# Biases ahead of positions, batch 0's logits in the loop, the pick in two parts and projections by 128 rows, in a recurrence, top-k and attention kernel

## The reference

```
a = tanh(x @ WA.T); b = x @ WB.T            # 16 states
h_t = a_t * h_(t-1) + b_t                   # restarts every batch
g = sigmoid(x @ Wg.T + bg); dx = x @ WD.T + bD
x = layernorm(x + (h @ WC.T) * g + dx * (1 - g))

weights = x @ router_w + router_b           # one logit per token
the 511 tokens with the largest weights, in order of position:
  hn = rmsnorm(x_sel, ln1); q, k, v = hn @ wq, wk, wv; rope(q), rope(k)
  attention with 16 heads of 16, causal mask picked by row and by column
  x1 = x_sel + o @ wo; x2 = x1 + gelu(rmsnorm(x1, ln2) @ w1) @ w2
  row of out = x2 * weight
x = layernorm(x + out + x * (1 - selected))
```

## Time and profile before

| what | us |
|---|---|
| median of 3 runs | 549.7 (548.16 to 550.84) |
| profiled execution, its own time | 546.17 |
| its span, first to last instruction | 544.4 |
| PE busy, matmuls | 444.0 (82%) |
| DVE busy | 392.7 (72%) |
| ACT busy | 293.5 (54%) |
| POOL busy | 185.7 (34%) |

### The profile page before, as it was taken

One profiled execution on the slowest core, in us unless ns is written; L12 is line 12 of the kernel. 1 busy time (PEld: TensorE's weight loads), 2 busy tenths in 40 slices (PEclk: granted clock), 3 DMA queues, 4 the chain that ended last, 5 costly groups with the idle time before them and its releaser, 6 DMA issues.

```text
span 544.4 us, 10299 instructions
## 1 busy us (share of the span) xinstructions
PE 444.0 (82%) x3346; PEld 329.2 (60%) x3346; DVE 392.7 (72%) x1218; ACT 293.5 (54%) x612; POOL 185.7 (34%) x218
## 2 busy tenths in 40 slices
PE   0379999999999533379798999997998999996980
PEld 0258778888888322345575666674585666673560
DVE  0357798888888788729568999947567999946050
ACT  1234546555564440024776999945577999942300
POOL 8015767676767650275940000001000000001432
PEclk9979999999999855559898999999999999998995
DMA  9601332424331210066650000000000000000100
GB/s 248 193 0 40 120 114 78 153 80 125 108 107 48 78 39 1 20 225 235 224 148 2 1 4 0 1 2 2 0 1 1 2 3 0 2 1 1 40 23 17
DMA packets 29846, 33.85 MB, mean 62 GB/s; under 512 B 6340, under 2 KB 25448, under 8 KB 29800
## 3 DMA queue, kind: packets, MB, share of 16 engines
q1 hardware_dynamic: 23024, 24.78, 14.1%
q0 software_dynamic: 3520, 8.40, 5.1%
q10 hardware_dynamic: 3256, 0.10, 0.5%
HBM read 19.63 MB, written 13.63 MB: 61 GB/s over the span
## 4 chain that ended last, share of the span: by engine, by line
PE 44%; DVE 11%; issue 4%; ACT 4%; POOL 2%; POOLq 1%; DVEq 0%; ACTq 0%
PE ps L871 10%; PE ps L887 6%; PE ps L941 5%; PE ps L858 5%; PE ps L948 4%; PE ps L808 3%; PE ps L834 3%; PE ps L827 2%; PE ps L744 1%; PE ps L812 1%; DVE arena L1325 1%; DVE arena L1532 1%; PE ps L793 1%; PE ps L766 1%; DVE qk L1335 1%
## 5 line engine op out<-in xcount | busy, mean ns | idle before, releaser
L1133 ACT ACTIVATE arena<-arena,nmax 128x511 f32<-128x511 f32 x128 | 92.0, 720 | 8.0 <-DVE nmax L1532 7.3
L1532 DVE CUSTOM_DVE_ANT_0 arena<-ps,nmask 128x511 f32<-128x511 f32 x128 | 84.8, 683 | 0.5 <-DVE nmask L1475 0.2
L871 PE MATMUL ps<-ident,arena 128*128 128x128 f32 x512 | 79.7, 278 | 3.5 <-ACT big L391 1.1
L871 PEld LDWEIGHTS ps<-ident,arena 128*128 128x128 f32 x512 | 60.3, 142 | 24.7 <-ACT arena L1133 14.5
L623 POOL COPY arena<-v_sb 128x256 f32<-128x256 f32 (+1 forms) x8 | 3.2, 398 | 155.3 <-PE ps L887 155.3
L676 PE MATMUL ps<-wgd_hi,x_hi 128*128 128x512 f32 x128 | 51.6, 403 | 0.0
L391 DVE COPY big<-ps 128x512 f32<-128x512 f32 x64 | 44.0, 688 | 9.9 <-PE ps L871 9.4
L858 PE MATMUL ps<-arena 96*128 (+1 forms) x128 | 49.3, 391 | 1.8 <-DVE nmask L1475 0.8
L678 PE MATMUL ps<-wgd_hi,x_lo 128*128 128x512 f32 x128 | 50.5, 395 | 0.0
L677 PE MATMUL ps<-wgd_lo,x_hi 128*128 128x512 f32 x128 | 50.4, 394 | 0.0
L485 POOL TENSOR_TENSOR arena<-arena 128x512 f32<-128x512 f32 x32 | 41.3, 1292 | 5.4 <-DVE arena L1226 3.6
(11 more groups left out here) (230 smaller groups left out, 1015.5 us busy)
## 6 DMA issues: line engine op xcount, KB each, us to landing
arena<-in_L_attn_x SPq DMA_DIRECT2D x16, 512.0 KB, 4.5
out<-ob_sb SPq DMA_DIRECT2D x16, 512.0 KB, 3.2
w_sb<-in_L_ffn_w SPq DMA_DIRECT2D x2, 1024.0 KB, 11.1
mt_scratch<-nmask SPq DMA_DIRECT2D x8, 256.0 KB, 2.6
mt_scratch<-big SPq DMA_DIRECT2D x8, 256.0 KB, 2.2
big<-in_L_attn_Wg SPq DMA_DIRECT2D x1, 256.0 KB
big<-in_L_attn_WD SPq DMA_DIRECT2D x1, 256.0 KB
wqk<-in_L_ffn_wq SPq DMA_DIRECT2D x1, 256.0 KB, 8.0
```

What stands on the lines that cost most here:

```text
L871: mm = pe.transpose(ps[:, 2 + u % 2, k * P:(k + 1) * P], pr[u % 4][:, k * P:(k + 1) * P], ident[:, :])
L1133: act.activation(pr[u % 4][:, 0:K - 1], sm[u % 4][:, 0:K - 1], ACT.Exp, bias=nmax[:, c, h:h + 1], scale=-1.0, accum_out=rsum[:, c, h:h + 1 ...
L1532: dve.tensor_tensor_reduce(sm[u % 4][:, 0:K - 1], ps[:, S_BANKS[u % AHEAD], 0:K - 1], nmask[b][:, c, 0:K - 1], 1.0, 3.4e38, ALU.add, ALU.m ...
```

## The change

It has these parts (line numbers are those of before):

- The four bias transfers get a semaphore of their own and stand right behind `WC` in ACT's queue; PE's first weight transposes wait for seven transfers. Positions are loaded by ACT in group 1 of the loop, between `round_h(2)` and `gate(1, 1)`.
- `recurrence_inputs(0)` stands ahead of tile 1's transposes; DVE splits the weights in four wider instructions, makes `scan(0)` ahead of the constants and the low part of tile 1's second half behind them; group 0's `gates` stand ahead of tile 2's transposes.
- `positions` moves from group 2 to group 6; batch 0's `logits` (DVE, end of group 9), `factors` (POOL, group 9) and `split_values` (POOL, group 10) stand in the loop.
- `pick` is cut in `pick_rows` (2 of 15 values) and `pick_rest` (13); `rows` needs the first alone, a new `factors` on DVE takes the rest. `pick_rest(1)` stands between PE's first and second projected chunk.
- Normalising, turning and projecting go chunk by chunk from each gather on. Batch 1's first two chunks are projected between the two batches' mask rows, which are turned through four banks.
- Two of ACT's four split copies go to POOL (`more_copies`), and POOL's queue behind the row and mask row gathers becomes as in the diff.
- Some pairs of semaphores become one that counts on.

```diff
 # POOL
-                if G == 2:
+                if G == 6:
                     positions()
+                if G == NG + 1:
+                    factors(0)
+                if G == NG + 2:
+                    split_values(0)
...
-            for b in range(B):
-                factors(b)
-            for b in range(B):
-                split_values(b)
+            factors(1)
+            split_values(1)
...
+            def more_copies(b, c):
+                q, k = (e_sb[c % 2][:, m, :, :, :] for m in range(2))
+                pool.wait_ge(e_parts, 2 * (c + b * C) + 2)
+                pool.tensor_copy(q[:, :, 1, :], q[:, :, 3, :])
+                pool.tensor_copy(k[:, :, 2, :], k[:, :, 3, :]).then_inc(e_ready[2], 1)
...
             gather_x(1)
             gather_mask_rows(1)
+            for c in range(2):
+                more_copies(0, c)
+            gather_mask_columns(0)
+            for c in range(2, C):
+                more_copies(0, c)
+            gather_mask_columns(1)
             for b in range(B):
                 first_sum(b)
             for b in range(B):
                 kept(b)
-            for b in range(B):
-                pool.wait_ge(mT_stored[b], 16 * M_STORES)
-                for c in range(C):
-                    gather(m_k[b][:, c, :], mt_dram[b], row_t[:, b, c:c + 1], m_k_in[b])
 # PE
+                if G == 0:
+                    pe.wait_ge(split_ready, 2 * KD + 1)
+                    pe.wait_ge(const_ready, 1)
                 pe.wait_ge(h_lo_ready, G + 1)
...
-            pe.wait_ge(w_loaded, 16 * 11)
+            pe.wait_ge(w_loaded, 16 * 7)
...
-            for b in range(B):
-                pick(b)
+            pick_rows(0)
+            pick_rest(0)
+            pick_rows(1)
...
-            turn_hn(0, 0)
-            project(0, range(C))
+            turn_first_hn(0, 0)
+            turn_first_hn(0, 1)
+            project(0, range(1))
+            pick_rest(1)
+            for c in range(1, C):
+                if c + 1 < C:
+                    turn_first_hn(0, c + 1)
+                project(0, range(c, c + 1))
             turn_mask_rows(0)
+            for c in range(2):
+                turn_first_hn(1, c)
+            for c in range(2):
+                project(1, range(c, c + 1))
+                turn_first_hn(1, 2 + c)
             turn_mask_rows(1)
-            turn_hn(1, 0)
...
             for c in range(C):
                 turn_split(0, c)
-                project(1, range(c, c + 1))
+                if c < 2:
+                    project(1, range(2 + c, 3 + c))
 # ACT
+                if G == 1:
+                    load_positions()
                 if G < NGB:
                     gate(G, 1)
...
-                    act.wait_ge(e_parts, 2 * done + 2)
-                    act.copy(q[:, :, 1, :], q[:, :, 3, :])
-                    act.copy(k[:, :, 2, :], k[:, :, 3, :]).then_inc(e_ready[1], 1)
 # DVE
+                if G == NG + 1:
+                    logits(0)
...
             angles(0)
-            dve.wait_ge(x_sel_in[0], 16 * C)
-            first_normalised(0)
+            for c in range(2):
+                first_normalised(0, c)
+            rows(1)
+            for c in range(2, C):
+                first_normalised(0, c)
+            factors(1)
             cosines(0)
             for c in range(C):
                 value(0, c)
                 rope(0, c)
-            dve.wait_ge(x_sel_in[1], 16 * C)
-            dve.wait_ge(hnT_done[0], KD)
-            first_normalised(1)
-            split(0, lambda c: value(1, c))
+                if c == 0:
+                    angles(1)
+                if c == 1:
+                    parts(0, 0)
+                if c == 2:
+                    for n in range(C):
+                        first_normalised(1, n)
+            parts(0, 1)
+            for c in range(2):
+                value(1, c)
+            for c in range(C):
+                copy_turned(0, c)
+                if c < 2:
+                    parts(0, 2 + c)
+                    value(1, 2 + c)
             copy_mask()
```

More of the change, by code:

```diff
@@ L626, in _ @@
                 all_turns(pool, turn_body)
-                rsqrt(ms[b][:, 5, :], ms[b][:, 4, :], ms_ready[b], 1, rms_ready[b])
+                rsqrt(ms[b][:, 5, :], ms[b][:, 4, :], ms_ready, b + 1, rms_ready)
+                if b < B - 1:
+                    for c in range(C):
+                        more_copies(b + 1, c)
             for b in range(B):
@@ L820, in turn_split @@
                 done = c + b * C
-                for n in range(2):
+                for n in range(3):
                     pe.wait_ge(e_ready[n], done + 1)
@@ L1036, in normalise, with load_positions @@
                 last.then_inc(ob_ready, 1)
+            def load_positions():
+                with nc.allow_non_contiguous_dma("positions by token"):
+                    for b in range(B):
+                        act.dma_start(pos_tok[:, b, :], pos_in[b].rearrange("(n p) -> p n", p=P)).then_inc(pos_loaded, 16)
+                        act.dma_start(pos_last[:, b, :], pos_in[b:b + 1, MS - 1:MS].broadcast_to((P, 1))).then_inc(pos_loaded, 16)
             copy_xT(0, 0)
@@ L1044, in _ @@
                 act.copy(wgd_hi[:, c, :], ps[:, 3 + c, :]).then_inc(wt_copied, 1)
-            for c in range(KD):
-                copy_xT(1, c)
+            copy_xT(1, 0)
             decays(0)
+            copy_xT(1, 1)
             round_h(0)
@@ L1304, in _ @@
[L1304 removed]
             def logits(b):
+                dve.wait_ge(dve_step, step.k)
                 step.link(dve.scalar_tensor_tensor(q1[:, b, :], minus_mean[:, b, :], sum_rw[:, :], dots[:, b, :],
@@ new lines, in _ @@
+            for c in range(KD):
+                dve.wait_ge(wt_copied, c + 2)
+                dve.tensor_tensor(wgd_lo[:, c, :], ps[:, 3 + c, :], wgd_hi[:, c, :].bitcast(F32),
+                                  ALU.subtract).then_inc(split_ready, 1)
+            rest_of_x(1, 0)
+            scan(0)
+            step.link(dve.tensor_reduce(is_lo[:, 0:1], ident[0:HROWS, N:2 * N], X, ALU.add))
+            step.done(dve.tensor_scalar(is_lo[:, 1:2], is_lo[:, 0:1], -1.0, 1.0, ALU.mult, ALU.add))
+            step.link(dve.tensor_tensor(wc_lo[:, :], ps[0:HROWS, 5, 0:D], wc_hi[:, :].bitcast(F32), ALU.subtract))
@@ new lines, in _ @@
+            dve.tensor_scalar(wc_d[0:HROWS, D:2 * D], wc_r[0:HROWS, :].bitcast(F32), -1.0, None,
+                              ALU.mult).then_inc(const_ready, 1)
+            rest_of_x(1, 1)
+            dve.wait_ge(router_loaded, 32)
+            dve.tensor_copy(ps[:, 1, 0:D], rw_row[:, :])
+            step.done(dve.tensor_reduce(sum_rw[:, :], rw_row[:, :], X, ALU.add))
+            for G in range(NGB + 1):
+                if G > 0:
+                    products(G - 1, 1)
+                    half_statistics(G - 1, 0)
+                if G + 2 < NGB:
+                    rest_of_x(G + 2, 0)
+                if G > 0:
+                    statistics(G - 1)
+                if G < NGB:
+                    products(G, 0)
+                if G + 2 < NGB:
+                    rest_of_x(G + 2, 1)
+                if G + 1 < NGB:
+                    scan(G + 1)
+                if G == NG + 1:
+                    logits(0)
@@ L1406, in _ @@
             one_hots(1)
-            rows(1)
+            factors(0)
             def mean_square(b, sums, out_):
@@ new lines, in copy_turned, with parts @@
+            def copy_turned(b, c):
+                for half in range(2):
+                    dve.wait_ge(eT_done[2 + half], c + b * C + 1)
+                    dve.tensor_copy(qkT[1][:, 8 * half:8 * half + 8, c * P:(c + 1) * P],
+                                    ps[:, :, :].bitcast(BF16)[0:ER, 2 + half, :].rearrange(
+                                        "r (h n) -> r h n", h=8)).then_inc(kT_ready, 1)
+            def parts(b, c):
+                done = c + b * C
+                dve.wait_ge(rope_ready[b], c + 1)
+                for n in range(4):
+                    if done >= 2:
+                        dve.wait_ge(eT_done[n], done - 1)
+                src = qk[b][:, c:c + 1, :].rearrange("p o (m h k) -> p (o m) h k", m=2, h=H)
+                es = e_sb[c % 2]
+                rest = e_rest[:, c % 2, :].rearrange("p (m h k) -> p m h k", m=2, h=H)
+                dve.tensor_copy(es[:, :, :, 0, :], src).then_inc(e_parts, 1)
+                dve.wait_ge(e_parts, 2 * done + 1)
+                step.link(dve.tensor_tensor(rest, src, es[:, :, :, 0, :], ALU.subtract))
+                dve.tensor_copy(es[:, :, :, 3, :], rest).then_inc(e_parts, 1)
+                dve.wait_ge(e_parts, 2 * done + 2)
+                step.done(dve.tensor_tensor(es[:, 0, :, 5, :], rest[:, 0], es[:, 0, :, 3, :], ALU.subtract))
+                dve.tensor_tensor(es[:, 1, :, 4, :], rest[:, 1], es[:, 1, :, 3, :],
+                                  ALU.subtract).then_inc(e_ready[0], 1)
```

347 lines of the change are left out of this document (166 added, 181 removed).

## The result

| | kernel before | changed kernel |
|---|---|---|
| median, us | 549.34 (548.16 to 550.84, 4 runs) | 552.84 (552.28 to 554.89, 4 runs) |
| ratio, 95% interval | | 1.0086 [1.0051, 1.0120] |
| profiled execution, own time / span | 546.17 / 544.4 | 554.89 / 552.6 |

The changed kernel is 3.5 us slower, where 1.6 us faster was forecast: inside the range of 538 to 557, on the wrong side.

What follows compares the result with a forecast made beforehand. PE was taken to bound the loop, chains of small steps the choice and projections. Terms -14.5 + 3.3 + 2.5 - 0.5 + 7.6 = -1.6 us gave 544.6 profiled, 548.1 us median; own range 544.5 to 551.5, overall 538 to 557.

Steps and rivals of the forecast that it cites:

- Start: Kernel start: weights no longer wait for biases and inputs are reordered; -14.5 us (ends -9 and -17).
- The order within the start: Start: first recurrence inputs no longer behind tile 1's transposes; L682 of group 1 at 43.0 instead of 47.08, 4.1 sooner.
- The feared 0.9 of clock: Start: more gaps on PE may put its clock at half again, 0.9 us off the gain.
- Positions in ACT: Loop group 1: ACT's four position issues delay the gate and copies PE needs; +3.3 us (ends 0 and 6.9).
- The groups in the loop: Loop groups 9 and 10: batch 0's logits, factors and value parts cost +2.5 us (ends 0 and 4.2).
- Pick: Row choice: pick_rows at 72 ns a matmul, 1.6 us sooner; pick_rest(1) some 2.1 us, with factors(1) waiting for it.
- Rival D: Pick: pick_rows bound by its 8 columns only, weight loads hidden; 1.5 us sooner than the sum, 546.6 us; chance 0.15.
- Part 5: Projections to attention: POOL's rearranged queue delays L871 from 292.67 to 300.3; +7.6 us (ends +3.5 and +14.2).
- rival B: Ahead of attention: POOL's chain later still, +14.2 us, total 554.7; decides if L871 starts behind 304.6; chance 0.18.
- rival C: Start gives less: WC lands only at 12.9, 4.7 us later than taken; total 552.8 us; chance 0.10.
- the 0.5 behind the loop: Behind the loop: batch 1's logits no longer wait for batch 0's; -0.5 us (ends 0 and -2).

Runs made afterwards that it cites:

- start_alone: Kernel before with only the loads changed (biases ahead, positions loaded by ScalarE in group 1, read in group 6): 0.9848 of the kernel before, 543.12 us.
- loop_out: Changed kernel with logits(0), factors(0) and split_values(0) back behind the loop: 0.9987 of the kernel before, 549.59 us.
- chip E: Later session, no hold: kernel before 544.76 us, the unaltered changed kernel 1.0000 of it.
- chip A: The chip of the first comparison, with a hold: kernel before 549.34 us, changed kernel 1.0086 of it.
- before_fourth: Kernel before, unaltered, run again on a chip with a hold: 550.27 us.
- before_third: Kernel before, unaltered, run again on a chip without a hold: 545.27 us.
- before_again: Kernel before, unaltered, run again on a chip without a hold: 543.96 us.
- late_out: Changed kernel with POOL's multiplies behind the first v_cur copy and batch 0's three steps behind the loop: 0.9724 and 0.9713 without a hold, 0.9844 with one.

## Why the prediction was wrong, point by point

1. *Start.* Forecast -14.5, measured -11.3 at group 1's L709: **3.2 us mis-sized**. WC landed at 9.4, not 8.2, which is 1.2 of it. The order within the start was reckoned at 4.1 and gave 1.5 (start_alone against the changed kernel): 3.6 at the first bias product, and then the two products of group 0 lie 7.5 us apart (24.30 to 31.82) where 5.4 lay before, more given back than the 1.9 taken. The feared 0.9 of clock did not come. (The clock's slices don't show where PE is busy, as the prediction read them: in the first, PE did nothing and the clock stood at 0.9.)
2. *Positions in ACT.* Forecast +3.3, measured +1.5 (the lead over before shrinks from 11.3 to 9.8 us at the next `scales`, 49.08 against 58.91 of the earlier trace rows). In group 1, with the start's loads done, even the long two issues took 0.45 and 0.60.
3. *The groups in the loop.* Forecast +2.5, measured +4.3: 2.8 in the group of `logits(0)` and `factors(0)` instead of 0.7, 1.5 in that of `split_values(0)` (1.8 forecast). loop_out gives 3.9 of it back. The changed kernel in that group, in order of time:

```profile
119.68 1.35 DVE L1326 SCALAR_TENSOR_TENSOR q<-minus_mean,sum_rw,dots 128x32 f32<-128x32 f32 x1
...
119.70 1.28 POOL L489 TENSOR_TENSOR arena<-arena 128x512 f32<-128x512 f32 x1
...
121.68 1.31 POOL L548 TENSOR_TENSOR h_parts<-arena,h_parts 16x512 fp32r<-16x512 f32 x1
...
121.88 1.15 DVE L1335 TENSOR_TENSOR qk<-Wf,qk 128x32 int32<-128x32 int32 x1
```

DVE's L1326 ends at 121.03 and L1335 at 123.03, each just behind the end of the POOL instruction beside it (120.98 and 122.99). Behind the loop the same L1335 took 0.19 and L1326 0.25 (L1333 and L1324 of loop_out). So two of DVE's small steps stood for 2.1 us in all, some half of the 4.3, and DVE was not as idle as its waits for PE let one think. That is read from the rows; no run takes these two waits alone away. The Trainium skill states this (SBUF — State Buffer, "SBUF: two separate sides"): the port pair of the two engines is locked for a whole instruction, also by a VectorE operation with two SBUF inputs against GpSimd's that read SBUF. The trace agrees for the two rows beside GpSimd's operations of 512 columns. It doesn't for one of 8: in loop_out the same two-input operation took 0.19 us at 180.35, inside GpSimd's L498 (179.52, 1.64 us).

4. *Pick.* 32 matmuls with 8 columns took 2.24 us, 70 ns each; 72 were taken. Rival D's rule is out. But `pick_rest(1)` took 3.5 us (230.46) where 2.1 were taken, **1.4 mis-sized**: the 2.1 counted on full clock, and its 52-column matmuls took 109 ns each at a granted clock of 1.00 and 108 at 0.50 (`pick_rest(0)`, 3.47 us in all). The first gather came 1.9 us sooner against the loop's end (-7.0 against -5.0, chip E).
5. **This is the step that failed.** Part 5 let DVE's `factors(1)`, and with it all ropes, wait for `pick_rest(1)` and priced that at the pick's own length, +2.1 us; that the announcement itself could come 8.8 us late was put at nothing. It put the end of chunk 3's second cast at 277.9 in the clock of the kernel before, 2.7 us sooner than 280.57. On chip A it ended at 278.7, which is 284.5 in that clock (5.84 us of lead at the loop's end): 6.6 too late. The hold is what stands in between. Without it, on chip E, the cast came 4.5 us sooner against the loop's end than before, and 2.7 were reckoned. What followed was as forecast: 21.7 us from that cast's start to L916 on chip E and on chip A alike (22.4 from its end were reckoned), with the multiplies at 0.9 each, and PE idle 9.54 (chip A) and 11.94 (D and E). In the clock of the kernel before, L916 started at 305.8 on chip A, behind the 304.6 at which rival B was to decide: **rival B happened**, through a cause that it did not name, and not through a busy DVE, since both groups of eight multiplies took 7.2 and not 9.4. That its 554.7 stood 1.9 above the measured time is luck, and so is that rival C's 552.8 is the measured time: WC landed at 9.4, not at C's 12.9.

Taken without the hold, the errors cancel: start and loop 3.7 us dearer than forecast (-5.0 at the loop's end against -8.7), the way to attention 2.5 cheaper (+4.6 against the loop's end, +7.1 reckoned with the 0.5 behind the loop). The forecast was -1.6 us; -0.4 of span and a ratio of 1.0000 and 1.0005 were measured on E and D. The sum was made on a trace without a hold, of a kernel whose median lay 3.5 us above it. before_fourth, with a hold, is 5.0 and 6.3 us slower than before_third and before_again; that the 3.5 was the hold fits this but has no trace, and the chip of the profiled execution is not on record.

## What to carry to other kernels

Before a queue is rearranged, write down what is behind each moved instruction and who needs it first: 14 us of multiplies that nobody waited for stood ahead of a 0.1 us memset that attention needed, and moving them behind it was worth 11.5 of the 15 to 17 us by which late_out beats the changed kernel. A median that lies some us above the profiled execution can be a sign that timed and profiled runs differ in something a single trace doesn't show, and here traces of the same kernel from a second chip told more than four edits on one. And be wary of a stage whose longest chain hangs on one announcement made beside a row of indirect gathers: that is where it was held here.

## What the runs showed of the hardware that was not expected

- On chips B and F and in the first comparison the semaphore of `pick_rest(1)`, a TensorE matmul's, raised beside GpSimd's indirect gathers, reached the waiting engines 2.8 to 3.1 us behind the end of the last row gather (six traces), 6.5 to 15.5 us after the matmul that raises it. On C, D and E the wait ended 0.03 to 0.05 us behind it beside the same gathers (eight traces). The kernel before has medians of 549.3 to 550.3 on the first three and 544.3 to 544.8 on the others, the changed one 552.8 and 544.6.
- Other announcements of TensorE beside gathers came 0.04 to 0.09 us behind the matmul in the same traces (233.52 on F, 229.85 on A), and TensorE's own eight matmuls took 7.7 us in place of 2.7 while the hold lasted (A and D).
- The clock was granted at 0.54 between 239 and 249 us behind the hold, and at 1.00 in the same kernel without one.
- Small issues in ScalarE's queue took 0.39 to 0.60 us in group 1, and up to 3.57 behind the start's other loads.
- Matmuls with 128 rows and strided operands took 70 ns with 8 columns and 122 with 60, both at a granted clock of 0.5. With 52 columns they took 108 at 0.5 and 109 at 1.0: the clock made no difference.
- A VectorE operation on 32 elements a row with two SBUF inputs took 1.15 us beside a GpSimd operation on 512 columns of 1.31 us, and 0.19 behind the loop, there even inside one on 8 columns of 1.64 us.
